# Delta rule: the keys multiply the state inside the recurrence, and four chunks pass the levels of the inverse in a rolling order

## The reference

```python
beta = sigmoid(x @ Wb) * 2.0
alpha = exp(-exp(A_log) * softplus(x @ Wa + dt_bias))
q, k, v = (silu(causal_dw_conv4(x @ W)) for W in (Wq, Wk, Wv))
q, k = l2norm(q), l2norm(k)
def step(state, t):                      # state: 64 x 128 per head
    retained = state @ k_t
    state = a_t * (state - b_t * outer(retained, k_t)) + b_t * outer(v_t, k_t)
    return state, state @ q_t
out = rms_normalised(out) * o_norm_w * silu(x @ Wg)
return out @ Wo                          # x = x + this
```

## Time and profile before

| | us |
|---|---|
| median of three runs | 3805.78 |
| the profiled execution | 3808.81 |
| its span | 3806.2 |
| TensorE busy in it | 3262.9 |
| VectorE busy in it | 2396.6 |
| delta stage, from its first projection to its last residual | 1713.2 to 3284.1 |

### The profile page before, as it was taken

One profiled execution on the slowest core, in us unless ns is written; L12 is line 12 of the kernel. 1 busy time (PEld: TensorE's weight loads), 2 busy tenths in 40 slices (PEclk: granted clock), 3 DMA queues, 4 the chain that ended last, 5 costly groups with the idle time before them and its releaser, 6 DMA issues. The chain is left out here.

```text
span 3806.2 us, 52445 instructions
## 1 busy us (share of the span) xinstructions
PE 3262.9 (86%) x18666; PEld 2525.1 (66%) x18666; DVE 2396.6 (63%) x5801; ACT 1356.5 (36%) x2713; POOL 158.4 (4%) x158
## 2 busy tenths in 40 slices
PE   5999938888999999747989898989898989488887
PEld 2665524445999999714867686868686869355554
DVE  6788425554777777766685858576767673354542
ACT  2333202221444444314534444444444442033232
POOL 0000000015111111000000000000000000000000
PEclk8999958999999999968797988888888886588786
DMA  1000080022899989741011111110111100100000
GB/s 62 23 17 12 11 160 12 11 75 81 305 322 317 320 318 323 253 152 64 34 34 35 34 36 34 35 34 35 34 35 34 35 20 1 53 12 23 12 17 12
DMA packets 203686, 327.31 MB, mean 86 GB/s; under 512 B 37449, under 2 KB 157522, under 8 KB 202258
## 3 DMA queue, kind: packets, MB, share of 16 engines
q1 hardware_dynamic: 196930, 305.94, 24.4%
q0 software_dynamic: 6480, 17.77, 1.2%
HBM read 275.15 MB, written 48.50 MB: 85 GB/s over the span
## 5 line engine op out<-in xcount | busy, mean ns | idle before, releaser
L767 PE MATMUL ex_ps<-ex_xbT,ex_w 128*128 128x128 f32 x4544 | 531.2, 275 | 1.7 <-DMA ex_b<-in_b_all_dram 1.2
L767 PEld LDWEIGHTS ex_ps<-ex_xbT,ex_w 128*128 128x128 f32 x4544 | 524.3, 192 | 6.1 <-DMA ex_b<-in_b_all_dram 1.8
L1378 PE MATMUL de_ps<-de_hT,de_w 128*128 128x512 f32 x640 | 306.2, 636 | 27.6 <-DMA de_w<-in_w_kqv_dram 13.9
L896 ACT ACTIVATE ex_t<-ex_ps,ex_b 128x128 f32<-128x128 f32 x568 | 208.8, 368 | 337.0 <-PE ex_ps L767 319.1
L1378 PEld LDWEIGHTS de_ps<-de_hT,de_w 128*128 128x128 f32 x640 | 129.0, 207 | 188.1 <-issue 186.0
L711 PE MATMUL ex_ps<-ex_xT,ex_w 128*128 128x512 f32 x512 | 230.6, 607 | 12.5 <-DVE ex_gl L1008 9.1
L1008 DVE SCALAR_TENSOR_TENSOR ex_gl<-ex_ps,ex_b,ex_t 128x128 f32<-128x128 f32 (+1 forms) x316 | 123.7, 391 | 137.3 <-ACT ex_t L896 69.4
L711 PEld LDWEIGHTS ex_ps<-ex_xT,ex_w 128*128 128x128 f32 x512 | 98.0, 195 | 131.8 <-issue 115.0
L1735 DVE SCALAR_TENSOR_TENSOR de_ya<-de_kx,de_taps,de_ya 128x512 f32<-128x512 f32 x192 | 142.5, 751 | 49.2 <-ACT de_ya L1574 44.7
L1008 DVE SCALAR_TENSOR_TENSOR ex_gm<-ex_ps,ex_b,ex_t 128x128 f32<-128x128 f32 (+1 forms) x316 | 121.8, 385 | 48.9 <-ACT ex_t L869 46.6
L177 PE MATMUL mx_ps<-mx_hT,mx_w_in 128*128 128x512 f32 x320 | 143.6, 605 | 8.3 <-ACT mx_hT L249 8.3
(11 more groups left out here) (378 smaller groups left out, 6268.3 us busy)
## 6 DMA issues: line engine op xcount, KB each, us to landing
ex_w<-in_w_all_dram SPq DMA_DIRECT2D x144, 1024.0 KB, 6.5
ex_w<-in_w_all_dram SPq DMA_DIRECT2D x72, 512.0 KB, 8.6
de_w<-in_w_kqv_dram SPq DMA_DIRECT2D x80, 256.0 KB, 2.8
de_ab<-alpha_d SPq DMA_DIRECT2D x8, 2048.0 KB, 8.3
ex_xb<-ex_xs_d SPq DMA_DIRECT2D x71, 129.0 KB
ex_xs_d<-ex_blank SPq DMA_DIRECT2D x71, 128.5 KB, 8.3
ex_w<-ex_y_d SPq DMA_DIRECT2D x16, 512.0 KB, 6.1
mx_xin<-in_x_dram SPq DMA_DIRECT2D x8, 512.0 KB, 4.0
```

What stands on the lines that cost most here:

```text
L767: m = pe.matmul(ps[:, n % 4, x * BLK:(x + 1) * BLK], w[:, k, part * HID + c * P:part * HID + (c + 1) * P], xbT[sx][:, k, :], start=(k == 0 ...
L896: act.activation(t1[:, n % 2, 0:BLK], ps[:, n % 4, 0:BLK], ACT.Identity, bias=b13[s][:, 0, n:n + 1]).then_inc(t1_ready, 1)
L1378: m = pe.matmul(ps[:, n % 2, :], w[:, g % SLOTS, k, n % 2 * P:(n % 2 + 1) * P], hT[:, k, :], start=(k == 0), stop=(k == KT - 1))
```

## The change

- **No pre-multiplied keys.** The scaling of the keys, their product with the inverse and its copy (kcg, L1614; L1500; WT, L1646) go. In the scan, chunks 1 to 3 multiply the keys by the state (K S), VectorE scales that and adds it to vb (`add_state`), and only then U = X vb is taken. Chunk 0 has a zero state: its state products are left out, and first state and first output are copies.
- **Value projections and Gram matrices** of b move between the scan steps of pb.
- **The inverse** goes chunk by chunk in a rolling order, each level of a chunk beside another level of the next; VectorE's convolutions are spread between, five inside the inverse and seven behind it.
- The squares for the output norm move to ScalarE, the query norm to the front of VectorE's body. The key tiles kx are double, Xc lies in vb (cleared by GpSimd in each batch), xin in o (loaded late).
- **The loops** are written out: eight bodies stand one behind another on each engine.

The core of the diff (the same edits of waits and of bank numbers throughout are left out):

```diff
-            def scan(pb):
...
-                    for hd in range(H):
-                        m = pe.matmul(ps[:, bank, hd * V:(hd + 1) * V], WT[:, c, hd, :], ST[:, hd, :],
-                                      start=False, stop=True, skip_group_check=True)
...
+                def with_state(c):
+                    pe.wait_ge(s["st"], pb * (NC - 1) + c)
+                    for hd in range(H):
+                        m = pe.matmul(ps[:, 3, hd * V:(hd + 1) * V], kc(pb, hd, c), ST[:, hd, :], start=True, stop=True, skip_group_check=True)
+                    m.then_inc(s["ks"], 1)
+                    pe.wait_ge(s["od"], pb * NC + c)
...
+                    m.then_inc(s["qs"], 1)
+                    pe.wait_ge(s["vs"], pb * (NC - 1) + c)
+
+                def state_step(c):
+                    pe.wait_ge(s["ud"], pb * (NC - 1) + c + 1)
...
+                u_products(0)
+                value(0)
+                state_step(0), outputs(0)
+                value(1)
+                with_state(1), u_products(1)
+                value(2)
+                state_step(1), outputs(1)
+                value(3)
+                with_state(2), u_products(2)
...
+                    gram_kk(pb, b, 0)
+                state_step(2), outputs(2)
...
+                    gram_kk(pb, b, 1)
+                with_state(3), u_products(3)
...
+                    gram_kk(pb, b, 2)
+                outputs(3)
...
+                    gram_kk(pb, b, 3)
...
-                    for c in both:
-                        pe.wait_ge(s["x6"], b * NC + c + 1)
-                        pe.wait_ge(s["kcg"], b * NC + c + 1)
-                        bank = 6 if c % 2 == 0 else 2
-                        for hd in range(H):
-                            m = pe.matmul(wide(bank)[:, hd, :], kcg[:, c % 2, hd, :], XT[:, c, hd, :], start=True, stop=True, skip_group_check=True)
-                        m.then_inc(s["wp"], 1)
+                y5(0), y5(1), x5(0), y5(2), x5(1), y5(3)
+                x11(0), x5(2), x11(1), y6(0), x5(3), x11(2), y6(1)
+                x6(0), x11(3), y6(2), x6(1), y6(3), x6(2), x6(3)
...
+                        query_norm()
+                        for n in range(6):
+                            conv(n)
+                        dve.wait_ge(s["cl_ld"], 32 * pb + 32)
+                        decay_u(0)
+                        conv(6)
+                        first_state()
+                        conv(7)
+                        first_out()
+                        decay_state(1)
...
+                    y5(0), y5(1)
+                    conv(8)
+                    y5(2)
+                    conv(9)
+                    y5(3)
+                    conv(10)
+                    y6(0)
+                    conv(11)
+                    y6(1)
+                    conv(12)
+                    y6(2), y6(3)
+                    conv(13)
+                    values(0), values(1)
+                    conv(14)
+                    values(2), values(3)
+                    for n in range(15, CONV):
+                        conv(n)
```

More of the change, by code:

```diff
@@ L1302, in stage_delta @@
         pair = lambda c: 2 + 2 * (c % 2)
+        gram = lambda c: 0 if c % 2 == 0 else 6
+        steps = [(b - 1 if b else None, b if b < BATCH else None) for b in range(BATCH + 1)]
         @block.sync
@@ new lines, in x6 @@
+                def x6(c):
+                    pe.wait_ge(s["y6"], b * NC + c + 1)
+                    pe.wait_ge(s["x5"], b * NC + min(c + 3, NC))
+                    if c >= 2:
+                        pe.wait_ge(s["x6"], b * NC + c - 1)
+                    for hd in range(H):
+                        m = pe.matmul(ps[0:HALF, 4 + c % 2, hd * HALF:(hd + 1) * HALF], Y6[HALF:P, c % 2, hd, :], XT[HALF:P, c, hd, HALF:P],
+                                      start=True, stop=True, skip_group_check=True)
+                    m.then_inc(s["x6p"], 1)
@@ L1544, in body @@
                     tail(b)
-            body(None, 0)
-            with pe.Fori(0, BATCH - 1) as pb:
-                body(pb, pb + 1)
-            body(BATCH - 1, None)
+            for pb, b in steps:
+                body(pb, b)
         @block.scalar
@@ L1599, in diagonals @@
                     act.wait_ge(s["dg"], b * NC + 2 * p + 2)
+                    if p == 0 and not first:
+                        act.wait_ge(s["os"], pb * NC + 1)
                     for q in range(NQ):
@@ L1773, in body @@
-                if not first:
-                    cB.start(pb)
-                    cD.start(pb)
-                    dve.memset(ST, 0.0).then_inc(s["st"], 1)
-                if b is not None:
-                    for n in range(5):
-                        conv(n)
-                if not first:
-                    dve.wait_ge(s["cl_ld"], 32 * pb + 32)
-                    decay_state(0), decay_u(0)
-                if b is not None:
-                    conv(5)
-                if not first:
-                    new_state(0), out_a(0)
@@ L1800, in body @@
-                if b is not None:
-                    decay(3, 6)
-                if not first:
-                    new_state(2), out_a(2), out_b(2)
-                if b is not None:
-                    decay(6, H)
-                if not first:
-                    out_a(3), out_b(3)
-                    cB.end()
-                if b is not None:
-                    for c in range(NC):
-                        dve.wait_ge(s["gk"], b * NC + c + 1)
-                        dve.tensor_tensor(DG[:, c, :, :], wide(pair(c)), ab[:, :, c * C:(c + 1) * C], ALU.mult).then_inc(s["dg"], 1)
```

436 lines of the change are left out of this document (238 added, 198 removed).

## The result

The changed kernel takes 3868.07 us (median of four executions, 3850.37 to 3882.85) against 3805.29 of the kernel before on the same chip: ratio 1.016, 95% interval 1.012 to 1.021. It is slower. The profiled execution is the fastest of the four, 3850.37 us, with a span of 3848.5 against 3806.2 and a mean granted clock of 0.836 against 0.864.

The account below looks back on a forecast made before the run. TensorE and VectorE were taken as nearly balanced, with the granted clock deciding much. Seven bodies +47, first -1.6, last -9.7 sum to +36 on 3808.81, 3845; the median lies 3.0 lower, 3842 us; range 3765 to 3950.

Parts of the forecast that it names:

- no loop edge: Between bodies: writing out the loops removes the issue idle and half clock behind it; 4.7 us taken, bounds 0 to 5.
- tail: From the query-key products to the body's end: 14.3 us before, starts at half clock, costs 1.7 more (13 if it stays down).
- First state step: Start of scan: TensorE idles 3.8 us for VectorE's decay at +21.0; clock falls until +31.4, costing 5 us.
- Last Gram matrix's end: End of the scan's remaining groups, value projections and Gram groups, at +67.1; interleaving brings Gram matrices back by 6 us.
- Half clock through the inverse: TensorE idles 5 to 8 us before the inverse, so its levels run at half clock: 46.4 us for four chunks.
- stretch: From the inverse's first product to the query-key products: 64.2 us, 56.6 before; bounds 43.5 and 64.2.
- Last body: Final body: 17 scan groups instead of 19 at half clock, short VectorE waits, norm work moved away; -9.7 us.
- The first body: First body: slower inverse and convolutions, tail 1.7 more, block chain some 6 us earlier; -1.6 us.
- rival C: Tail stays at half clock, next key projections start slow: body 207, kernel 3943 us; chance 0.19.
- A: Clock comes back inside the inverse: stretch about 46.5, body 176.3, kernel 3718 us; chance 0.10.
- B: TensorE does not idle before the inverse, only Y6 and X6 at half: stretch 55, kernel 3778 us; chance 0.13.
- D: Waits cancel within 0.2%: body 187 to 190, kernel 3798 to 3813 us; chance 0.08.

Follow-up runs that it names:

- E3: Changed kernel, order only: ten VectorE convolutions inside the inverse instead of five, two among the value scalings; 3839 us, 1.010 of the kernel before.
- E5: Changed kernel, order only: second query-key group moved ahead of the tail's first one-column products; 3895 us, 1.019 of the kernel before.
- E7: Changed kernel plus 7 filling products of 128x512 on constants before the inverse (10 in the first body); median 3862 us (3811 to 3906), no ratio given.
- E9: Changed kernel plus 6 filling products of 128x512 before the query-key products alone; 3838 us, 1.007 of the kernel before.
- E8: Changed kernel with the order moves of E3, E4 and E5 and the filling products of E7; 3762 us, 0.985 of the kernel before.
- E11: E10 with seven more filling products between the inverse's level groups, and three instead of six before the tail; 3663 us, 0.963 of the kernel before.
- E4: Changed kernel, order only: first decay of the new values after five convolutions instead of six; 3818 us, 1.003 of the kernel before.
- E2: Changed kernel plus 32 key products of 128x128, result unread, put back at the inverse's end; 4008 us, 1.054 of the kernel before.
- E10: Changed kernel with order moves of E3 and E4, old tail order, filling products wherever TensorE would wait; 3700 us, 0.970 of the kernel before.
- E12: Kernel before the change, loop kept, with filling products of 128x512 where TensorE waits in its inverse; 3714 us, 0.976 of the kernel before.

## Why the prediction was right

3842 us was forecast, slower, with 0.69; 3868 was measured, 3850 in the profiled execution.

*Steps that held.* Key projections 13.8 us, no loop edge, except behind the slow first tail (16.2 there). First state step at +21.0 (+21.0 forecast) after 3.5 us of waiting (3.8), groups and value projection at half clock, back at +30.7 (+31.4). Last Gram matrix's end at +66.9 (+67.1). TensorE done at +106.5 (+106 to +109), inverse at +113.1 (+113.8), idle 6.6 (5 to 8). Half clock through the inverse, stretch 64.8 (64.2). Body 193.6 in the mean (194.0). Seven bodies 1355.1 us against 1310.8: +44 (+47); in each the inverse starts some 4 us earlier than before the change, the stretch is 8.2 longer and the tail some 1.8. Last body 86.1 us against 96.4: -10.3 (-9.7).

*The term that was mis-sized.* The first body: 174.1 us (1710.75 to 1884.86) against 163.7, +10.4, where I had -1.6. The step was the tail, "if the clock is back after about 3.5 us of 128x128 products, it costs 1.7; if it stays down through the alternation with one-column products, 13. I take 1.7". In the first body it stayed down and cost 13. That is rival C, which I had as one case for all bodies, while it goes body by body. The sum of the profiled span is 44.3 + 10.4 - 10.3, less 2.5 for a stage that began earlier and 0.4 more behind it: +42.3, which is 3848.5 - 3806.2.

*The other 18 us.* The median lies 18 above the profiled execution. E3, E5 and E7 show tails of 16 and of 21 to 27 in one and the same execution, and E9, which warms them, has the spread shrink from 32.5 to 13 us. So further half-clock tails are the likely cause of 3868 and 3883, whose mean clocks are 0.831 and 0.827; without profiles of those executions this is argued, not shown.

*Are they the causes?* Filling the idle time before the inverse gave 11 to 12 us of stretch per body with nothing else changed (E7), so the clock there is a cause; it was the mechanism that the prediction let decide. Moving VectorE's convolutions gave 11.8 as well at half clock (E3). They don't add (51.3 together, E8): TensorE, at full clock, then waits for the convolutions, and its clock falls within the inverse; with the clock held there too the stretch is 44.4 (E11). The start of the scan is worth 2 to 3.5 us of the inverse's start (E4), less than the 5 that I priced, though the half clock behind the wait did cost some 5 us in the changed kernel (12.1 us from the state step's start to the first query-state group, four groups at 1.77 otherwise); a second wait stood behind the first.

*The rivals.* A, the clock coming back by itself in the inverse: in no body of any run. E2 and E5 show groups of 128x128 that bring it back, and E7 and E10 that 64-row groups without a gap don't even keep it. The Trainium skill, TensorE: Matmul & The Clock Gate, "What's actually happening", says that activity releases the throttle; by that rule, if busy time were meant, E10 should have kept the clock, and the trace does not agree. B, no idling before the inverse: E7 makes that case by other means; the gain in the stretch was the one of B (55 forecast there, 52.7 to 53.7 measured), but not the total, since E7's tails were slow in four bodies of eight.

C came in part, in the first body, as said. D, that the waits cancel, asked for a body of 187 to 190.

## What to carry to other kernels

Taking work from TensorE where another engine sets the end does not only gain nothing: the idle time can halve the clock of the products behind it, here 6.6 us of waiting, which made the stretch behind it 11 to 12 us longer. Price a change by the clock that each stretch will start with, and try dense products in TensorE's waits, and between small products, before reordering anything; they must be sized so as to end just ahead of what they wait for. A change in order is judged with the stretch behind it: E3 gained 11.8 us and gave 12.2 back behind it.

## What the runs showed that I had not expected

- A gapless run of products can lose the clock (E10: 0.98, then 0.50, TensorE busy for 18.0 of 18 and 23.0 of 23 us), and 3.6 us of one-column products in a row can (E5), though they need not (E8). In turn with 128x128 groups the same products were seen at full from end to end (14.3 us for the tail), at half from end to end (27.5), rising (3.78, then 2.03 in the changed kernel's looped tails) and falling (2.77, then 3.76 in E3).
- A pause's length is no guide: 14.16 us came before tails of 27.5 and of 16.3 in one execution. Nor did the runs find a length between the prediction's 1.60 and 3.97 us that decides: the clock fell behind 1.87 us in E4, and behind 1.55 us and one fast group in E8.
- The last scan's groups follow each other without a gap at half clock in the kernel before and at full in E12. What set the one going slow and the other fast is open.
- A looped body remembers the clock of the one before: a half-clock tail moves the next inverse from +113.1 to +115.7 (E7), and E7 and E8 alternate between two kinds of body.
- The changed kernel with the loop kept was not tried (its key tiles alternate by the batch's parity), nor the fillings of E11 without its moves of order.
